# A sixteen-sublayer model in one kernel: when the semaphores of its stages are cleared

## What is computed

```
x = x + _L0_attn_a_ref(_layernorm(x, axis=-1), ...)   # running mean
x = x + _L0_ffn_ref(_layernorm(x, axis=-1), ...)      # 8 experts, top 2, softmax gates
x = x + _L0_attn_b_ref(_layernorm(x, axis=-1), ...)   # causal attention with rotary tables
...
x = x + _L2_attn_b_ref(_layernorm(x, axis=-1), ...)   # attention, 16 heads
x = x + _L2_ffn_ref(_layernorm(x, axis=-1), ...)      # dense layer with low-rank experts
x = x + _L3_attn_a_ref(_layernorm(x, axis=-1), ...)   # local attention + linear attention on 7 levels
x = x + _L3_ffn_ref(_layernorm(x, axis=-1), ...)
x = x + _L3_attn_b_ref(_layernorm(x, axis=-1), ...)   # attention with a filter on q and k
x = x + _L3_ffn_ref(_layernorm(x, axis=-1), ...)
return x
```

## Time and profile before

| | us |
|---|---|
| median of 3 runs | 5682.81 |
| lowest, highest | 5679.38, 5686.02 |
| the profiled execution | 5680.1 |
| its span (first to last instruction) | 5678.3 |
| PE busy in the span | 4648.3 |
| DVE busy | 3369.8 |
| ACT busy | 2530.4 |
| POOL busy | 986.6 |

### The profile page before, as it was taken

One profiled execution on the slowest core, in us unless ns is written; L12 is line 12 of the kernel. 1 busy time (PEld: TensorE's weight loads), 2 busy tenths in 40 slices (PEclk: granted clock), 3 DMA queues, 4 the chain that ended last, 5 costly groups with the idle time before them and its releaser, 6 DMA issues. The chain is left out here.

```text
span 5678.3 us, 66434 instructions
## 1 busy us (share of the span) xinstructions
PE 4648.3 (82%) x22439; PEld 1716.3 (30%) x22489; DVE 3369.8 (59%) x4929; ACT 2530.4 (45%) x4600; POOL 986.6 (17%) x896
## 2 busy tenths in 40 slices
PE   6949999794069999757599997687777959999889
PEld 3422222342033333233122222264443421222244
DVE  4346555335964555243788883336884359888543
ACT  2325555233004434312388884242222327888733
POOL 0000000000007878800000000134660000000000
PEclk8969999897579999968699998798997979999989
DMA  1010000000000000000100000110000010000000
GB/s 57 19 61 31 31 30 18 16 15 0 0 7 3 5 3 5 18 12 0 56 30 24 28 20 2 45 62 3 1 1 12 19 50 23 29 26 24 10 19 19
DMA packets 43295, 118.21 MB, mean 21 GB/s; under 512 B 13768, under 2 KB 14792, under 8 KB 41960
## 3 DMA queue, kind: packets, MB, share of 16 engines
q1 hardware_dynamic: 40432, 113.17, 5.8%
q0 software_dynamic: 2560, 1.19, 0.1%
HBM read 89.61 MB, written 19.01 MB: 19 GB/s over the span
## 5 line engine op out<-in xcount | busy, mean ns | idle before, releaser
L857 DVE TENSOR_REDUCE 72_heads_mx<-72_heads_mps 128x1 f32<-128x1024 f32 x512 | 602.2, 1218 | 83.7 <-PE 72_heads_mps L736 82.5
L857 DVE TENSOR_REDUCE 45_heads_mx<-45_heads_mps 128x1 f32<-128x1024 f32 x512 | 602.4, 1218 | 83.1 <-PE 45_heads_mps L736 81.9
L831 ACT ACTIVATE 45_heads_p<-45_heads_sps 128x512 f32<-128x512 f32 x1024 | 552.9, 596 | 111.6 <-PE 45_heads_sps L757 108.0
L831 ACT ACTIVATE 72_heads_p<-72_heads_sps 128x512 f32<-128x512 f32 x1024 | 552.8, 596 | 111.7 <-PE 72_heads_sps L757 108.1
L857 DVE TENSOR_REDUCE 9_heads_mx<-9_heads_mps 128x1 f32<-128x1024 f32 (+7 forms) x384 | 332.9, 908 | 244.1 <-PE 9_heads_mps L739 238.2
L1687 ACT ACTIVATE 30_latent_heads_p<-30_latent_heads_ring 128x512 f32<-128x512 f32 x512 | 277.3, 594 | 386.0 <-PE 30_latent_heads_ring L1606 374.6
L1705 DVE TENSOR_REDUCE 30_latent_heads_mx<-30_latent_heads_ring 128x1 f32<-128x512 f32 x512 | 322.9, 684 | 199.9 <-PE 30_latent_heads_ring L1586 199.9
L831 ACT ACTIVATE 9_heads_p<-9_heads_sps 128x512 f32<-128x512 f32 (+3 forms) x640 | 314.2, 532 | 233.4 <-PE 9_heads_sps L760 126.3
L757 PE MATMUL 45_heads_sps<-45_heads_qs,45_heads_ks 123*128 123x512 bf16 x1024 | 310.9, 386 | 5.1 <-ACT 45_heads_p L831 5.1
L757 PE MATMUL 72_heads_sps<-72_heads_qs,72_heads_ks 123*128 123x512 bf16 x1024 | 310.6, 385 | 5.2 <-ACT 72_heads_p L831 5.2
L1562 POOL TENSOR_TENSOR 30_latent_heads_psum<-30_latent_heads_psum,30_latent_heads_p 128x1024 f32<-128x1024 f32 x112 | 264.1, 2358 | 87.8 <-ACT 30_latent_heads_p L1687 87.8
(11 more groups left out here) (906 smaller groups left out, 7381.1 us busy)
## 6 DMA issues: line engine op xcount, KB each, us to landing
56_local_heads_qs<-scratch_q_parts SPq DMA_DIRECT2D x48, 96.0 KB
56_local_heads_ks<-scratch_k_parts SPq DMA_DIRECT2D x48, 96.0 KB
4_experts_wbuf<-in_L0f_experts SPq DMA_DIRECT2D x8, 514.0 KB
12_experts_wbuf<-in_L0f_experts SPq DMA_DIRECT2D x8, 514.0 KB
66_experts_wbuf<-in_L3f_experts SPq DMA_DIRECT2D x8, 514.0 KB
75_experts_wbuf<-in_L3f_experts SPq DMA_DIRECT2D x8, 514.0 KB
9_heads_qs<-scratch_q_parts SPq DMA_DIRECT2D x32, 96.0 KB
9_heads_ks<-scratch_k_parts SPq DMA_DIRECT2D x32, 96.0 KB
```

The costliest lines, as they stand in the source:

```text
L831: act.activation(pslot[x % PS][:, 0:CW - off], sps[e % SB][:, 0:CW - off], ACT.Exp, scale=SCALE / 2).then_inc(ex_done, 1)
L857: dve.tensor_reduce(mx[h % 2][:, i, half:half + 1], mps[x % 2][:, 0:w], AX.X, ALU.max).then_inc(mx_taken, 1)
```

## The change

`Stage.__enter__` no longer enters `cleanup_on_exit`. The stage still gives back its buffers, but its semaphores stay taken. `build` wraps `cleanup_on_exit` around the first norm and around the call of each sublayer instead. Within a sublayer every stage so gets semaphores with new numbers; at the sublayer's end one clear covers the numbers of all of its stages, and one barrier follows. The barrier at the end of each `Block` stays.

```diff
@@ Stage @@
     def __enter__(self):
-        self.stack.enter_context(self.nc.cleanup_on_exit())
         return self
@@ build @@
         g.last = False
-        residual_and_norm(g, first=True)
+        with nc.cleanup_on_exit():
+            residual_and_norm(g, first=True)
         for n, sublayer in enumerate(SUBLAYERS):
             g.last = n == len(SUBLAYERS) - 1
-            sublayer(g)
+            with nc.cleanup_on_exit():
+                sublayer(g)
```

## The result

| | median us | runs | lowest, highest |
|---|---|---|---|
| before | 5681.6 | 4 | 5679.4, 5686.0 |
| with the change | 5652.3 | 4 | 5643.3, 5658.1 |

The ratio is 0.995 with a 95% interval of 0.9937 to 0.9963: 29 us less by the medians, 21 to 36 us less by the interval. The forecast was 24.4 us less, 5658.4. (The kernel before has one run more here than in its table of times, which moves its median from 5682.8 to 5681.6.)

A forecast was written before the change was run, and what follows sets the result against it. The prediction saw a chain of stages with no single limiting engine, so pauses between stages add to the span. Fixed parts 23.1 us plus late arrivals 1.3 make 24.4 off 5682.8: 5658.4 us, range 5650 to 5667.

The forecast's parts named there:

- What bounds the time: Between stages all engines stand still; time there adds to the span whatever engine bounds the stages beside it.
- The number: Stage ends: of 77 cleanups 60 go, 53 with a clear and 7 that are a barrier alone.
- The price of one: Per cleanup at a stage end: 0.35 us for a barrier alone, 0.39 with a clear, plus 0.0068 for each semaphore.
- The part that stays: Clearing the same 554 semaphores in 17 portions still costs 3.8 us; the 102 of `hale_attention` make a cleanup of some 1.1.
- rival 4: Large clears cost twice the slope, 3.8 us more, giving 5662 us; its chance is included in the forecast's 0.86.
- Late arrivals: At some cleanups one engine takes its next instruction late; 2.6 us at removed places, half taken as gained, 1.3 us.
- fixed parts: Share of the 60 removed cleanups that goes: 53 x 0.39 and 7 x 0.35, together 23.1 us.
- Rival 1: Removed barriers had covered the fetch of the next stage's code; 19.8 us come back, 5678 us; chance 0.05.
- Rivals 2 and 3: TensorE's clock at stage starts: returns later, 5694.8 us, chance 0.01; or shifts some 10 us net, 5648 or 5669, chance 0.08.

The follow-up runs named there:

- barrier_only: Changed kernel with an all-engine barrier, without a clear, put back at the end of each of 77 stages: 24.6 us over the changed kernel on the same chip.
- barriers_at_start: Kernel before with 77 more all-engine barriers in one place, behind the cleanup of the first norm: 27.1 us slower than the kernel before.
- second_barrier: Kernel before with one more all-engine barrier behind each of its 77 cleanups: 40.5 us slower than the kernel before, 40.7 when repeated.
- clear_behind: Changed kernel without its 17 cleanups; POOL alone clears, no barrier behind, numbers held until the next sublayer ends: 36.9 us faster than the kernel before, 37.0 when repeated.
- third_barrier: Kernel before with two more all-engine barriers behind each of its 77 cleanups: 62.5 us slower than the kernel before.

## Why the prediction was right

- **What bounds the time.** That whole-core pauses add to the span whatever engine is the limit inside the stages: shown by barrier_only and barriers_at_start, in which 77 barriers cost 24.6 and 27.1 us where 77 x 0.33 = 25.4 was to be expected. second_barrier, at 40.5 us, is the exception: there something came on top of the pauses.
- **The number.** 60 cleanups, 53 of them with a clear: the traces show 77 and 17 cleanup barriers, 70 and 17 clears.
- **The price of one.** The stage end of the earlier trace rows went from 0.82 to 0.29 us, as said.
- **The part that stays.** The 17 cleanups were put at 17 x 0.39 + 3.8 = 10.4 us and took 10.5; the clear of 102 at 0.62 us and it took 0.587; its cleanup at 1.1 and it took 1.37 - 0.28 = 1.09. The line from 3 to 25 semaphores held up to 102, so rival 4 falls.
- **Late arrivals.** This is the term that was sized wrong. I had counted 2.6 us of them at the removed places and taken half as gained. The gaps fell by 25.6 us, 2.5 us more than the fixed parts' 23.1, so nearly all of it left the gaps. Whether it came back inside blocks can be seen only where PE does nothing, since there the clock does not blur the sum. Of these twelve blocks eight have the length of before to 0.02 us; the other four vary by 0.3 us and more from trace to trace. In the PE-heavy blocks 0.2 us cannot be told from the clock. So up to 2.5 us were gained and not 1.3. That a late arrival goes with the number of instructions passed and not with a barrier has two pieces of evidence. In both traces of second_barrier two of the quiet blocks are longer, 9.10 us instead of 8.69 and 5.41 instead of 5.13, at the same two places, where the added instructions may have moved it. And the late arrival of the earlier trace rows is gone in the changed kernel, although the cleanup there stays and its clear is longer:

```profile
4570.47 0.60 ACT L159 ACTIVATE nT<-67_norm_fwd 128x512 f32<-128x512 f32 x1 [0.64 <-PE 67_norm_fwd L111]
4571.88 0.28 PEld L200 LDWEIGHTS 69_qk_bank<-nT,weights_L3b 128*128 128x128 f32 x1 [1.86 <-issue]
```

That is 4571.88 - 4571.07 = 0.81 us instead of 0.93. That it is a wait for the instruction stream was argued, and no run tested it.
- **Rival 1** (the pause covers code fetch, 5678 us) had 0.05. Where a pause was added or removed at all stages the time followed it, and the 0.28 us between two blocks is now found where cleanups were removed, as the 0.29 us above shows for one. In the changed trace the first busy instruction of a block, on whichever engine, starts 0.12 to 0.25 us after the release at all places but four, and at these four (7.5, 4.4, 2.1 and 0.6 us) it is much the same in the trace of before (8.0, 4.2, 2.8 and 0.6 us). The Trainium skill (Runtime: NRT & Kernel Launch, instruction fetch mechanics) warns of a stall at a taken branch outside the fetched window; none of the 60 places shows a new one of the 0.33 us that this rival needs.
- **Rivals 2 and 3** (the clock). They were right about the mechanism, but not about its width. The price of 2.6 us holds for the low-rank experts' stage (88.9 and 86.3 us), while other blocks moved by more: 18_dt by 6.2 us in second_barrier, and the local head loop by 5.0 us between two traces of the changed kernel. For the noise I had taken 3.3 us, half the spread of three runs. The runs of the changed kernel spread over 15 us, and the lowest of them, 5643.3, lies outside the range that I gave for the median. The median, 5652.3, is 6.1 us under the forecast and 2.3 us inside the range; the gaps explain 1.2 us of that, and the rest is the spread of the runs. So the mechanism was right, and that so narrow a range held had some luck in it. That a kernel as a whole can lose more than its pauses is shown by second_barrier: 16 us, twice, with PE 13.5 and 19.6 us longer busy. In the direction of the change, shorter pauses, it did not.

## What to carry to other kernels

If a program has phases that end in a barrier of all engines, count the barriers first: each costs at least its time in full, here 0.33 us, and what a second one behind it protects (here the reuse of semaphore numbers) could here be had from a barrier that stands there anyway (clear_behind). Clearing costs mostly by the semaphore, 0.0065 us each, and little by the call, 0.39 - 0.35 = 0.04 us; what it saves to put clears together is above all their barriers. Compare gaps and block lengths apart in the trace: the gaps of the changed kernel repeat to 0.01 us in its three traces and those of second_barrier to 0.4 us, while the blocks vary by several us with TensorE's clock.

## What the runs showed of the hardware that I had not expected

- TensorE's granted clock follows a pattern that partly belongs to a kernel: two traces of second_barrier have PE busy at the low clock for 12.6 us in 18_dt and 7.9 in each of the norms 46 and 73; third_barrier has 0, 7.4 and 10.3 there, and every other trace 0 and 3.3 to 4.5. The local head loop does not repeat: 198.0, 193.0 and 193.4 us in three traces of the changed kernel.
- A clear of a range of semaphores is linear in their number over a wide stretch: 46 ns for 3, 174 for 25, 304 for 49, 587 for 102, so 5.5 ns each over the whole, and every engine waits for it when a barrier follows.
- The spread of single runs, 14 to 25 us for the kernel before within the later groups, is more than half of what this change is worth.
